# An eight-layer transformer stack: two bias products move from TensorE to VectorE, and the attention behind the expert layer is reordered

## The chip, the cores and the metric

One core of a Trainium2 chip runs the whole program. The metric is device microseconds of one execution, the median of several runs.

## The reference

x has 8 blocks of 128 rows by 512. Eight layers are added to it in turn, each on a layer norm of x. The change lies in the third (L1 attention) and in how it is prepared and started inside the second (L0 expert layer, 4 of 16 experts a row and one shared).

```python
x = x + _L0_xattn_ref(_layernorm(x), ctx_4096, mask, ...)
x = x + _L0_ffn_ref(_layernorm(x), ...)            # 16 experts, top 4, a shared expert
x = x + _L1_xattn_ref(_layernorm(x), ctx_4096, L1_xattn_Wq, L1_xattn_bq, L1_xattn_Wk, L1_xattn_bk)
...
def _L1_xattn_ref(text, features, Wq, bq, Wk, bk):
    Q = jnp.einsum('btx,dx->btd', text, Wq) + bq
    K = jnp.einsum('bpx,dx->bpd', features, Wk) + bk
    scale = 1.0 / jnp.sqrt(K.shape[-1])
    attn = jax.nn.softmax(jnp.einsum('btd,bpd->btp', Q, K) * scale, axis=-1)
    return jnp.einsum('btp,bpd->btd', attn, features)
```

## The kernel before

The function `l0_ffn` (L777) holds the expert layer and the L1 attention behind it, in one block with a hand-written order for each engine; semaphores tie them together. x stays in SBUF. On trn2's TensorE a product of exact f32 is written as one `pe.matmul` and shows as two instructions; elsewhere three products of split parts (`matmul_split`, L239) stand for one.

**Ahead of the loop.** The shared expert is computed (`job`, `down`), while VectorE routes rows: `send(b)` makes one-hot rows and `add(b)` (L1217) adds a block of the shared expert's result. `down` (L1490) waits for `add` of the block but one before and calls `join(c, d)` (L1589) after each block. Four joins, of four products each, make Wk^T Wq, 512 by 512, in PSUM banks 0 to 3; the first two run before `down`. `tokens` (L1534) turns the one-hots into lists; VectorE makes gather and scatter indices of them. `join_vec` (L1601) multiplies both weights with the other's bias: 72 matmuls of one column (Wk bq, Wq bk, bk bq); ScalarE takes them (`take_vec`). Then `tile_turn(0)` waits for rows gathered by GpSimd (`gather`, L1177).

**The tile loop.** 47 tiles of 128 rows of one expert each. Step t on TensorE: `tile_gu(t)` (12 split products), `tile_turn(t+1)`, `tile_down(t-1)` (L1577), `tile_turn_z(t)`. ScalarE: silu(t), the copy of turned rows t+1, the upper part of the weights of t+2 (`tile_gu_hi`, which waits for their load), the output of t-1. VectorE: z(t), rests of rows t+1, zt(t), rest of the weights of t+2 (`tile_gu_lo`), and from t = 21 on, in 18 steps, one step of the quantisation of the next layer's weights (`quantise_weights`, L1417). GpSimd gathers rows of t+3 and scatters picks of t-2. SP (L966 to L1021) issues all plain loads on one queue in the order below; `load_gu` is conditional: a tile with the expert of the one before loads nothing.

```python
for t in range(F0_BUFS, F0_TILES):      # F0_BUFS = 3, F0_TILES = 47
    load_gu(t)                          # 1 MB, waits for t_gu_lo_ready of t - 3
    if t > F0_BUFS: load_dn(t - 1)      # 0.5 MB, waits for t_y_done of t - 4
    if t == 2 * F0_BUFS: ...            # waits for the joins, then a_ct (2 MB, ctx_turned)
    if t == 4 * F0_BUFS: ...            # a_rows (2 MB, ctx_rows)
    if t == 6 * F0_BUFS: ...            # the next layer's weights and columns, 1.75 MB (prefetch)
```

**Behind the loop.** Keys of a half of the blocks are five products (`keys(n, c)`, n = 5 half + m; the fifth is the row of bias terms) of the joined matrix with ctx_turned. The five of half 0 come first. The four picks of each block are loaded into three 1 MB buffers, and `add_pick` adds them; statistics (`ahead.dve`), variance and power on GpSimd, `rows(b)` (the normalised block, two buffers), `turn_rows`, `scores`, `maxima`, `exponentials`, `turn_e`, `attend` (L1665), `add_attended` with the next norm's statistics. These run in a pipeline of ten steps; the 20 chunks of half 1's keys stand in its first four steps, five in each (`late_keys`), between the other work of TensorE. After the last rstd comes a barrier, then the next layer.

Of the kernel before, what the change touches and what calls it, by code (L numbers as in the profile page):

```python
# [12 lines left out]
B = 8  # L13
# [763 lines left out]
def l0_ffn(core):  # L777
    nc, dram, ps = core.nc, core.dram, core.psum
    with ExitStack() as lay:
# [149 lines left out]
        a_bias = sbuf(nc, lay, "a1_bias", [P, 2, NC])  # L929
# [4 lines left out]
        a_xn = t_dn[:, 2, :, :]  # L934
        a_row, a_ones = logit[0:1, :], before_f[0:1, P:2 * P]
        a_w_loaded = [core.sem(f"a1_w_loaded_{i}") for i in range(2)]
        a_bias_loaded, prefetched = core.sem("a1_bias_loaded"), core.sem("f0_prefetched")
        a_joined_done, a_joined_ready = core.sem("a1_joined_done"), core.sem("a1_joined_ready")
        a_vec_done, a_vec_ready = core.sem("a1_vec_done"), core.sem("a1_vec_ready")
# [8 lines left out]
        VEC_BANK, XT_BANK, JOB_BANK, S_BANK, ET_BANK, A_BANK = 7, 0, 2, 4, 5, 6  # L948
# [5 lines left out]
        with nc.Block(no_gpsimd_drain=True) as block:  # L954
            @block.sync
            def _(sp):
# [29 lines left out]
                sp.dma_start(a_bias[:, :, :], dram["a1_bias"]).then_inc(a_bias_loaded, 16)  # L986
# [9 lines left out]
                for t in range(F0_BUFS, F0_TILES):  # L996
# [3 lines left out]
                    if t == 2 * F0_BUFS:  # L1000
                        sp.wait_ge(a_joined_done, NC)
                        sp.wait_ge(a_vec_done, 1)
                        for h in range(HALVES):
                            sp.dma_start(a_ct[:, h, :, :].rearrange("p c n -> p (c n)"), dram["ctx_turned"][h])\
                              .then_inc(a_ct_loaded[h], 16)
                    if t == 4 * F0_BUFS:
# [3 lines left out]
                    if t == 6 * F0_BUFS:  # L1010
# [13 lines left out]
            def _(act):  # L1024
# [43 lines left out]

                def take_vec():

                    act.wait_ge(a_vec_done, 1)
                    act.mul(a_vec[:, 0:2 * NC], ps[:, VEC_BANK, 0:2 * NC], a_scale).then_inc(a_vec_ready, 1)
                    act.mul(a_vec[0:1, 2 * NC:], ps[0:1, VEC_BANK, 2 * NC:2 * NC + 1], a_scale)\
                       .then_inc(a_vec_ready, 1)
# [60 lines left out]
                take_vec()  # L1135
# [10 lines left out]
                for n in range(KEY_JOBS):  # L1146
                    take_keys(n)
                for s in range(1, B + 2):
                    if s >= 2:
                        exponentials(s - 2)  # L1150
                        take_turned(s - 2)
                    if s <= B:
                        take_rows(s - 1)
                    if s <= HB:
                        take_keys(KEY_JOBS + s - 1)
                    if s == HB:
                        take_keys(KEY_JOBS + s)

            @block.gpsimd
            def _(pool):  # L1160
# [39 lines left out]
                for s in range(B + 2):  # L1200
                    if s < B:
                        ahead.scale(pool, s)
                    if s >= 2:
                        late.scale(pool, s - 2)
# [4 lines left out]
            def _(dve):  # L1209
# [149 lines left out]
                def rows(b):  # L1359
# [3 lines left out]
                    if b >= 2:  # L1363
                        dve.wait_ge(a_turned, b - 1)
                    dve.tensor_scalar(a_xn[:, b % 2, :], core.x[:, b, :], ahead.mean(b), ahead.rstd(b),
# [49 lines left out]
                Q_FROM = 7 * F0_BUFS  # L1415
# [35 lines left out]
                for t in range(F0_TILES):  # L1451
# [4 lines left out]
                    if t + 2 < F0_TILES:  # L1456
                        tile_gu_lo(t + 2)
                    quantise_weights(t)
                for s in range(B + 2):
                    if s < B:  # L1460
                        dve.wait_ge(picks_loaded[s], 16)
                        add_pick(s, 0)
                        add_pick(s, 1)
                    if 1 <= s <= B:
                        rows(s - 1)
                    if s < B:
                        add_pick(s, 2)
                        add_pick(s, 3)
                        dve.wait_ge(picks_added, F0_TOPK * (s + 1))
                        ahead.dve(dve, s)  # L1470
                    if s >= 2:
                        add_attended(s - 2)
                    if 1 <= s <= B:
                        maxima(s - 1)
# [1819 lines left out]
```

## Time and profile before

| | us |
|---|---|
| median of 3 runs (1162.65 to 1171.52) | 1163.18 |
| the profiled execution | 1166.7 |
| its span | 1164.9 |
| TensorE busy in the span | 969.0 |
| VectorE busy | 723.1 |
| ScalarE busy | 459.6 |
| GpSimd busy | 393.1 |

The execution's time is taken around the span; the 1.8 us between them lie outside what the profile shows. Busy shares are means over stages with different bounds. Start times below count from the span's start. PE is TensorE, DVE VectorE, ACT ScalarE, POOL GpSimd, SP the engine that issues loads. In square brackets stands the idle time just before an instruction and what ended it.

### The profile page before, as it was taken

The page shows a single profiled execution, that of the slowest core. Times are in us where ns is not written, and L with a number is a line of the kernel's source. Part 1 is how long each engine was busy: PE and PEld are TensorE (multiplying, and loading weights), DVE is VectorE, ACT ScalarE, POOL GpSimd, SP SyncE. Part 2 cuts the span into 40 slices and gives each one's busy share as a digit, 9 for nine tenths or more (in the row PEclk, how much of TensorE's full clock was granted, in tenths as well). Part 3 has the DMA queues.
Part 4 walks back from the last instruction along what each step waited for, and adds up shares of the span by engine and source line. Part 5 has one row for each costly group of instructions (what it writes and reads, how often), then busy time and mean ns, then how long its engine had stood idle before and what let it go on. Part 6 is the DMA issues. An engine that isn't in the chain of part 4 may idle for free. (4 is left out here: it accounts for less than half of the span.)

```text
span 1164.9 us, 15202 instructions
## 1 busy us (share of the span) xinstructions
PE 969.0 (83%) x5083; PEld 643.6 (55%) x5083; DVE 723.1 (62%) x1183; ACT 459.6 (39%) x671; POOL 393.1 (34%) x355
## 2 busy tenths in 40 slices
PE   4888766999999999999734389899986588769997
PEld 2565533786666666654412168544463255457886
DVE  4767464675776778736859744477744667544434
ACT  2445323224666566632232143344402256335130
POOL 5334111213676666631112640100011231227531
PEclk8899675988999999999855579799988889979999
DMA  8000103134888866545100131000001020022000
GB/s 301 1 2 2 55 0 133 42 148 138 317 313 317 288 228 244 204 143 195 55 0 1 44 119 37 19 2 1 1 1 73 37 82 0 1 72 91 19 19 37
DMA packets 31982, 110.09 MB, mean 95 GB/s; under 512 B 4321, under 2 KB 4641, under 8 KB 28577
## 3 DMA queue, kind: packets, MB, share of 16 engines
q1 hardware_dynamic: 24384, 84.47, 20.0%
q0 software_dynamic: 7520, 24.65, 6.0%
q8 instruction: 42, 0.69, 0.2%
q14 instruction: 36, 0.29, 0.1%
HBM read 130.07 MB, written 16.78 MB: 126 GB/s over the span
## 5 line engine op out<-in xcount | busy, mean ns | idle before, releaser
L1186 POOL DMA_INDIRECT f_picks<-f_turn_xn,f_target x47 | 116.4, 2477 | 71.5 <-ACT f_turn_xn L1063 71.2
L1585 PE MATMUL banks<-f_t_dn,f_z 128*128 128x512 f32 x188 | 88.5, 593 | 0.6 <-issue 0.6
L1328 DVE TENSOR_TENSOR f_gu_lo<-f_t_gu,f_gu_hi 128x2048 fp32r<-128x2048 f32 x24 | 55.0, 2293 | 15.1 <-ACT f_gu_hi L1049 14.2
L1180 POOL DMA_INDIRECT f_turn_xn<-f_xn_rows,f_token x47 | 47.4, 1008 | 50.1 <-DVE f_token L1322 21.4
L106 POOL TENSOR_TENSOR a_ahead_var_eps<-mean_var,eps 128x1 f32<-128x1 f32 x24 | 4.8, 199 | 176.0 <-DVE mean_var L102 176.0
L1328 DVE TENSOR_TENSOR f_xn_lo<-f_t_gu,f_xn_hi 128x2048 fp32r<-128x2048 f32 x23 | 52.7, 2292 | 10.7 <-ACT f_xn_hi L1049 10.3
L2255 ACT ACTIVATE a_e<-banks 128x1024 f32<-128x1024 f32 x32 | 32.8, 1024 | 52.8 <-PE banks L2354 52.7
L1049 ACT CAST f_gu_hi<-f_t_gu 128x2048 fp32r x24 | 45.7, 1904 | 11.9 <-DMA f_t_gu<-in_f_gu 9.0
L1056 ACT ACTIVATE f_sil<-banks 128x256 f32<-128x256 f32 x47 | 18.1, 384 | 80.1 <-PE banks L244 80.1
L164 PE MATMUL banks<-ident,f_turn_xn 128*128 128x128 f32 x96 | 21.3, 374 | 33.9 <-DVE f_turn_xn L172 33.9
L100 DVE BATCH_NORM_STATS2 stat<-x_res 128x6 f32<-128x512 f32 x64 | 44.3, 692 | 5.5 <-DMA x_res<-in_x 3.5
L1049 ACT CAST f_xn_hi<-f_t_gu 128x2048 fp32r x23 | 43.7, 1901 | 7.2 <-DMA f_t_gu<-in_f_gu 5.1
L1585 PEld LDWEIGHTS banks<-f_t_dn,f_z 128*128 128x128 f32 x188 | 32.1, 190 | 23.3 <-issue 23.2
L453 ACT ACTIVATE a_e<-banks 128x1024 f32<-128x1024 f32 x32 | 31.0, 1021 | 35.4 <-PE banks L661 35.4
L421 POOL TENSOR_TENSOR a_k<-a_kf,a_k_sel 128x512 fp32r<-128x512 f32 x16 | 20.8, 1302 | 68.8 <-ACT a_k_sel L445 68.8
L2292 DVE TENSOR_REDUCE a_mx<-banks 128x8 f32<-128x1024 f32 x32 | 39.1, 1222 | 7.2 <-PE banks L2336 5.9
L242 PE MATMUL banks<-f_gu_hi,f_xn_hi 128*128 128x512 f32 x96 | 41.0, 427 | 1.9 <-issue 1.9
L542 DVE TENSOR_REDUCE a_mx<-banks 128x8 f32<-128x1024 f32 x32 | 37.6, 1218 | 5.3 <-PE banks L644 5.3
L1333 DVE TENSOR_TENSOR f_xn_lo<-banks,f_xn_hi 128x512 fp32r<-128x512 f32 x47 | 32.4, 690 | 11.9 <-ACT f_xn_hi L1041 11.5
L2368 PE MATMUL banks<-a_e,raw 128*32 128x512 f32 x128 | 35.4, 631 | 4.6 <-DVE a_ot_lo L2284 4.6
L242 PE MATMUL banks<-f_xn_hi 128*128 128x512 f32 x92 | 38.2, 415 | 1.0 <-issue 1.0
L243 PE MATMUL banks<-f_gu_lo,f_xn_hi 128*128 128x512 f32 x96 | 39.0, 406 | 0.0
(437 smaller groups left out, 2705.9 us busy)
## 6 DMA issues: line engine op xcount, KB each, us to landing
f_t_gu<-in_f_gu SPq DMA_DIRECT2D x47, 1024.0 KB
f_t_dn<-in_f_dn SPq DMA_DIRECT2D x47, 512.0 KB, 4.3
f_t_gu<-f_picks SPq DMA_DIRECT2D x8, 1024.0 KB, 5.4
f_xn_rows<-f_turn_xn SPq DMA_DIRECT2D x9, 256.0 KB, 2.5
x_res<-in_x SPq DMA_DIRECT2D x8, 256.0 KB, 8.3
a_ctx<-in_ctx SPq DMA_DIRECT2D x2, 1024.0 KB, 13.8
a_out_mask<-in_mask SPq DMA_DIRECT2D x1, 2048.0 KB, 16.0
a_ct<-in_ctx_turned SPq DMA_DIRECT2D x2, 1024.0 KB, 11.3
```

Source lines behind the costliest of these rows:

```text
L100: dve.bn_stats(self.stat[:, b, :], src).then_inc(self.stat_ready, 1)
L242: pe.matmul(out, w_hi, m_hi, start=start, stop=False)
L243: pe.matmul(out, w_hi, m_lo, start=False, stop=False)
L542: dve.tensor_reduce(mx[:, :, PAIR * (s % 2) + A0_MAX_ROW:PAIR * (s % 2 + 1):A0_SLOT].rearrange("p w r -> p r w"), ps[:, s_banks(s), :].rea ...
L1049: act.copy(t_gu_hi[t % 2], t_gu[:, bass.ds(i, 1), :, :].rearrange("p i c n -> p (i c n)"))\
L1180: pool.indirect_dma_start(t_rows[:, t % F0_BUFS, :], None, dram["f0_xn_rows"], bass.IndirectOffsetOnAxis(ap=token[:, t:t + 1], axis=0))\
L1186: pool.indirect_dma_start(dram["f0_picks_flat"], bass.IndirectOffsetOnAxis(ap=target[:, t:t + 1], axis=0), t_y[:, t % F0_BUFS, :], None).t ...
L1328: dve.tensor_tensor(t_gu_lo[t % 2], t_gu[:, bass.ds(i, 1), :, :].rearrange("p i c n -> p (i c n)"), t_gu_hi[t % 2].bitcast(F32), ALU.subtr ...
L1585: mm = pe.matmul(ps[:, TY_BANK + t % 2, :], t_zt[:, t % 2, c, :], t_dn[:, t % F0_BUFS, c, :], start=c == 0, stop=c == F0_IC - 1)
L2255: act.activation(e[:, u % 2, 2 * (s % 2):2 * (s % 2) + 2, :], ps[:, s_bank(s):s_bank(s) + 2, :], ACT.Exp, scale=scale).then_inc(exp_ready, 1)
L2292: dve.tensor_reduce(mx[:, tiles, A2_MAX_ROW:P:A2_SLOT].rearrange("p m r -> p r m"), ps[:, s_bank(s):s_bank(s) + 2, :].rearrange("p r (m j) ...
L2368: mm = pe.matmul(ps[A2_VSLOT * i:A2_VSLOT * (i + 1), O_BANK + u % 2, :], v[:, b // HB, b % HB, g * A2_PER_GROUP + i, :], e[:, u % 2, i, :] ...
```

## The change

- The bias products: SP loads both weights turned, wk and wq (1 MB each), into `raw`, and the two biases repeated over all partitions (0.5 MB) into the room of a_rows, all at t = 6 in front of a_ct. VectorE multiplies and sums in nine instructions (`join_biases`) in tiles t = 9 to 17. `join_vec` and `take_vec` go.
- The joins of chunks 2 and 3 move from `down` to behind `tokens`.
- a_rows is loaded at t = 21 instead of 12, once all nine are done; the prefetch at 21 instead of 18; the quantisation starts at t = 24 instead of 21.
- Behind the loop TensorE makes all ten keys in one go. VectorE adds the picks of six blocks meanwhile; `rows` has six buffers (all of t_dn) instead of two. Then come nine steps, the first eight of them with a block's scores.

```diff
@@ -926,17 +926,19 @@
         a_wk, a_wq = (core.raw[:, i, :].rearrange("p (c n) -> p c n", c=NC) for i in range(2))
-        a_bias = sbuf(nc, lay, "a1_bias", [P, 2, NC])
+        a_turned_w = core.raw[:, :, :].rearrange("p i (c n) -> p i c n", c=NC)
+        a_bias = a_rows[:, 0, 0:2, :]
         a_vec = sbuf(nc, lay, "a1_vec", [P, 2 * NC + 1])
...
         a_inv = sbuf(nc, lay, "a1_inv", [P, B])
-        a_xn = t_dn[:, 2, :, :]
+        a_xn = t_dn[:, :, :, :].rearrange("p i c n -> p (i c) n")
+        A_XN = F0_BUFS * F0_IC
...
@@ -983,7 +985,6 @@
 
-                sp.dma_start(a_bias[:, :, :], dram["a1_bias"]).then_inc(a_bias_loaded, 16)
                 sp.wait_ge(gu_lo_ready, 1)
...
@@ -999,15 +1000,18 @@
                         sp.wait_ge(a_joined_done, NC)
-                        sp.wait_ge(a_vec_done, 1)
+                        for i, w in enumerate(("a1_wk_turned", "a1_wq_turned")):
+                            sp.dma_start(core.raw[:, i, :], dram[w]).then_inc(a_turned_loaded, 16)
+                        sp.dma_start(a_bias, dram["a1_bias"]).then_inc(a_turned_loaded, 16)
                         for h in range(HALVES):
...
                               .then_inc(a_ct_loaded[h], 16)
-                    if t == 4 * F0_BUFS:
+                    if t == 7 * F0_BUFS:
+                        sp.wait_ge(a_vec_ready, 2 * NC + 1)
                         for h in range(HALVES):
...
                               .then_inc(a_rows_loaded[h], 16)
-                    if t == 6 * F0_BUFS:
+                    if t == 7 * F0_BUFS:
                         for i, src in enumerate(core.upcoming):
...
@@ -1132,7 +1129,6 @@
                 tile_x(0)
-                take_vec()
                 for t in range(F0_TILES):
...
@@ -1143,18 +1139,14 @@
 
-                for n in range(KEY_JOBS):
+                for n in range(HALVES * KEY_JOBS):
                     take_keys(n)
-                for s in range(1, B + 2):
-                    if s >= 2:
-                        exponentials(s - 2)
-                        take_turned(s - 2)
-                    if s <= B:
-                        take_rows(s - 1)
-                    if s <= HB:
-                        take_keys(KEY_JOBS + s - 1)
-                    if s == HB:
-                        take_keys(KEY_JOBS + s)
+                take_rows(0)
+                for s in range(B):
+                    exponentials(s)
+                    if s + 1 < B:
+                        take_rows(s + 1)
+                    take_turned(s)
 
...
@@ -1197,11 +1189,13 @@
                 pool.drain()
-                for s in range(B + 2):
-                    if s < B:
-                        ahead.scale(pool, s)
-                    if s >= 2:
-                        late.scale(pool, s - 2)
+                for b in range(A_XN):
+                    ahead.scale(pool, b)
+                for s in range(B + 1):
+                    if s + A_XN < B:
+                        ahead.scale(pool, s + A_XN)
+                    if s >= 1:
+                        late.scale(pool, s - 1)
 
...
@@ -1360,9 +1354,9 @@
                         dve.wait_ge(t_y_done, F0_TILES)
-                    if b >= 2:
-                        dve.wait_ge(a_turned, b - 1)
-                    dve.tensor_scalar(a_xn[:, b % 2, :], core.x[:, b, :], ahead.mean(b), ahead.rstd(b),
+                    if b >= A_XN:
+                        dve.wait_ge(a_turned, b - A_XN + 1)
+                    dve.tensor_scalar(a_xn[:, b % A_XN, :], core.x[:, b, :], ahead.mean(b), ahead.rstd(b),
                                       ALU.subtract, ALU.mult).then_inc(a_xn_ready, 1)
...
@@ -1412,7 +1406,20 @@
 
-                Q_FROM = 7 * F0_BUFS
+                def join_biases(t):
+
+
+                    n = t - 3 * F0_BUFS
+                    if n == 0:
+                        dve.wait_ge(a_turned_loaded, 48)
+                    if 0 <= n <= 2 * NC:
+                        i, c = divmod(n, NC)
+                        one = a_turned_w[:, i, c, :] if i < 2 else a_bias[:, 0, :]
+                        dve.scalar_tensor_tensor(out=turned.xn[:, B - 1, :], in0=one, scalar=a_scale,
+                                                 in1=a_bias[:, min(i, 1), :], op0=ALU.mult, op1=ALU.mult,
+                                                 accum_out=a_vec[:, n:n + 1]).then_inc(a_vec_ready, 1)
+
+                Q_FROM = 8 * F0_BUFS
 
...
@@ -1455,23 +1462,28 @@
                         tile_gu_lo(t + 2)
+                    join_biases(t)
                     quantise_weights(t)
-                for s in range(B + 2):
+                def all_picks(b):
+                    dve.wait_ge(picks_loaded[b], 16)
+                    for k in range(F0_TOPK):
+                        add_pick(b, k)
+                    dve.wait_ge(picks_added, F0_TOPK * (b + 1))
+                    ahead.dve(dve, b)
+
+                all_picks(0)
+                for b in range(1, A_XN):
+                    all_picks(b)
+                    rows(b - 1)
+                for s in range(B + 1):
+                    if s + A_XN < B:
+                        all_picks(s + A_XN)
+                    if s + A_XN - 1 < B:
+                        rows(s + A_XN - 1)
                     if s < B:
-                        dve.wait_ge(picks_loaded[s], 16)
-                        add_pick(s, 0)
-                        add_pick(s, 1)
-                    if 1 <= s <= B:
-                        rows(s - 1)
-                    if s < B:
-                        add_pick(s, 2)
-                        add_pick(s, 3)
-                        dve.wait_ge(picks_added, F0_TOPK * (s + 1))
-                        ahead.dve(dve, s)
-                    if s >= 2:
-                        add_attended(s - 2)
-                    if 1 <= s <= B:
-                        maxima(s - 1)
+                        maxima(s)
+                    if s >= 1:
+                        add_attended(s - 1)
 
...
@@ -1500,7 +1512,6 @@
                         mm.then_inc(y_done, 1)
-                        join(2 + b // NC, b % NC)
 
...
@@ -1598,28 +1607,13 @@
 
-                def join_vec():
-
-
-                    pe.wait_ge(a_bias_loaded, 16)
-                    pe.wait_ge(sigmoid_ready, 1)
-                    for i, w in enumerate((a_wk, a_wq)):
-                        for c in range(NC):
-                            for d in range(NC):
-                                pe.matmul(ps[:, VEC_BANK, i * NC + c:i * NC + c + 1], w[:, d, c * P:(c + 1) * P],
-                                          a_bias[:, 1 - i, d:d + 1], start=d == 0, stop=d == NC - 1)
-                    for d in range(NC):
-                        mm = pe.matmul(ps[0:1, VEC_BANK, 2 * NC:2 * NC + 1], a_bias[:, 1, d:d + 1],
-                                       a_bias[:, 0, d:d + 1], start=d == 0, stop=d == NC - 1)
-                    mm.then_inc(a_vec_done, 1)
-
                 def keys(n, c):
...
                             pe.wait_ge(a_joined_ready, NC)
-                            pe.wait_ge(a_vec_ready, 2)
+                            pe.wait_ge(a_vec_ready, 2 * NC + 1)
                             pe.wait_ge(t_z_ready, F0_TILES)
...
@@ -1687,7 +1681,9 @@
                 tokens()
-                join_vec()
+                for c in range(2, NC):
+                    for d in range(NC):
+                        join(c, d)
                 pe.wait_ge(y_added, B)
...
@@ -1700,28 +1696,19 @@
 
-                for n in range(KEY_JOBS):
+                for n in range(HALVES * KEY_JOBS):
                     for c in range(NC):
                         keys(n, c)
-                def late_keys(s, a, b):
-
-                    if s <= HB:
-                        for i in range(KEY_JOBS * (s - 1) + a, KEY_JOBS * (s - 1) + b):
-                            keys(KEY_JOBS + i // NC, i % NC)
-
-                for s in range(1, B + 2):
-                    if s >= 2:
-                        turn_e(s - 2)
-                    late_keys(s, 0, 1)
-                    if s >= 2:
-                        attend(s - 2)
-                    late_keys(s, 1, 2)
-                    if s <= B:
-                        turn_rows(s - 1)
-                    late_keys(s, 2, 3)
-                    if s <= B:
-                        scores(s - 1)
-                    late_keys(s, 3, KEY_JOBS)
+                turn_rows(0)
+                for s in range(B + 1):
+                    if s < B:
+                        scores(s)
+                    if s + 1 < B:
+                        turn_rows(s + 1)
+                    if s >= 1:
+                        attend(s - 1)
+                    if s < B:
+                        turn_e(s)
         core.next = 1 - core.next
...
@@ -3175,7 +3162,8 @@
     out["a1_wk"], out["a1_wq"] = rows(a["L1_xattn_Wk"]), rows(a["L1_xattn_Wq"])
-    out["a1_bias"] = np.stack([a["L1_xattn_bk"].reshape(NC, P).T, a["L1_xattn_bq"].reshape(NC, P).T], 1)
+    out["a1_wk_turned"], out["a1_wq_turned"] = rows(a["L1_xattn_Wk"].T), rows(a["L1_xattn_Wq"].T)
+    out["a1_bias"] = np.broadcast_to(np.stack([a["L1_xattn_bq"], a["L1_xattn_bk"]]), (P, 2, D))
     out["f1_w"] = a["L1_ffn_W"].reshape(NC, P, D).transpose(1, 0, 2).reshape(P, NC * D)
...
         [a[f"L1_ffn_{key}"] for key in ("calib_min", "calib_max", "bias")]), (P, 3 * D))
```

## Rows read from the trace of the kernel before

**Rows 1.** The page: TensorE's clock in 40 slices of 29.1 us.
```profile
PEclk8899675988999999999855579799988889979999
```

**Rows 2.** Windows: us, each engine's busy us, then clock, DMA share, GB/s.
```profile
249.00:262.00 13.00, 13.00 (x102) 12.65 (x101) 6.16 (x9) 1.77 (x4) 4.73 (x3) 0.68 0.19 61
262.00:515.00 253.00, 248.34 (x1042) 170.63 (x1042) 180.20 (x205) 153.72 (x187) 158.09 (x90) 0.98 0.68 246
...
580.00:600.00 20.00, 10.98 (x43) 6.12 (x41) 8.49 (x20) 3.68 (x10) 3.68 (x10) 0.67 0.00 0
```

**Rows 3.** TensorE's timeline ahead of the loop: start us, us, line, operation.
```profile
248.52 1.02 PE L1596 MATMUL banks<-raw 128*128 128x512 f32 x2
249.38 1.56 PE L1538 MATMUL banks<-f_sent,f_at_row 128*128 128x94 bf16 x32
250.78 11.21 PE L1609 MATMUL banks<-a_bias,raw 128*128 128x1 f32 x64
...
262.19 1.12 PE L1550 MATMUL banks<-ident,f_turn_xn 128*128 128x128 f32 x4
264.75 0.77 PE L242 MATMUL banks<-f_gu_hi,f_xn_hi 128*128 128x512 f32 x1 [1.45 <-issue]
```

**Rows 4.** Timeline of VectorE and GpSimd there; landings of ten gathers.
```profile
246.48 0.69 DVE L1219 TENSOR_TENSOR x_res<-banks,x_res 128x512 f32<-128x512 f32 x1
...
248.72 0.69 DVE L1219 TENSOR_TENSOR x_res<-banks,x_res 128x512 f32<-128x512 f32 x1
...
253.27 1.24 POOL L1180 DMA_INDIRECT f_turn_xn<-f_xn_rows,f_token  x1 [21.39 <-DVE f_token L1322]
...
DMA to landing us min/median/max: 3.2/3.7/8.5
```

**Rows 5.** Windows of one us, clock before the DMA share.
```profile
270.00:271.00 1.00, 0.93 (x5) 0.65 (x3) 0.34 (x1) 0.42 (x2) 0.00 (x0) 0.67 0.00 0
```

**Rows 6.** Landings of a_ct's two loads, of load_dn(6), and TensorE's tile_down(6).
```profile
L1004 SPq DMA_DIRECT2D a_ct<-in_ctx_turned x2: 432/454/475, 288.5 to 289.0; - x2
...
DMA to landing us min/median/max: 9.3/11.3/13.2
...
L982 SPq DMA_DIRECT2D f_t_dn<-in_f_dn x1: 342/342/342, 293.2 to 293.2; - x1
...
DMA to landing us min/median/max: 11.2/11.2/11.2
...
306.63 1.88 PE L1585 MATMUL banks<-f_t_dn,f_z 128*128 128x512 f32 x4
```

**Rows 7.** VectorE's timeline at t = 21: a quantisation step, then z.
```profile
385.40 0.68 DVE L1395 TENSOR_REDUCE f_weights_scale<-raw 128x1 f32<-128x512 f32 x1
386.12 0.42 DVE L1341 TENSOR_TENSOR f_z<-f_sil,banks 128x256 f32<-128x256 f32 x1
```

**Rows 8.** Timeline of ScalarE at the loads of t = 24 and 25.
```profile
387.62 1.91 ACT L1049 CAST f_gu_hi<-f_t_gu 128x2048 fp32r x1 [1.74 <-DMA f_t_gu<-in_f_gu]
...
393.35 1.91 ACT L1049 CAST f_xn_hi<-f_t_gu 128x2048 fp32r x1 [2.04 <-DMA f_t_gu<-in_f_gu]
```

**Rows 9.** Timeline behind the loop, all engines.
```profile
515.24 13.90 PE L1632 MATMUL banks<-a_ct,a_joined 128*128 128x512 f32 x32
...
524.93 3.11 DVE L1355 SCALAR_TENSOR_TENSOR x_res<-f_t_gu,f_weight,x_res 128x512 f32<-128x512 f32 x4 [11.58 <-DMA f_t_gu<-f_picks]
...
528.07 0.69 DVE L100 BATCH_NORM_STATS2 stat<-x_res 128x6 f32<-128x512 f32 x1
...
573.83 2.04 PE L1654 MATMUL banks<-f_turn_xn,a_xt 128*128 128x128 f32 x8 [0.72 <-issue]
...
588.74 1.13 PE L1654 MATMUL banks<-f_turn_xn,a_xt 128*128 128x128 f32 x8 [0.72 <-issue]
...
589.80 0.48 PE L1656 MATMUL banks<-f_logit,f_before_f 1*128 1x128 f32 x2
...
596.09 0.54 POOL L109 TENSOR_TENSOR rstd<-second_ahead_var_eps,neg_half 128x1 f32<-128x1 f32 x1
```

## What the change was predicted to do

> **What bounds the kernel now.** First the page's slices, then one table of the windows of each stage, then the timeline of each place where the change cuts in. The clock row of the slices (29.1 us each) [rows 1] reads 8 from 233 to 291, 9 up to 553, then 8 and 5. The windows tell which work that is [rows 2]: in the loop (262 to 515) TensorE is busy 248.3 of 253 us at a clock of 0.98, with the DMA engines at 0.68. It is the bound there, but only because data comes in time. In 580:600 it is busy 11 of 20 us at 0.67, where steps wait on one another. In 249:262 it is "full", but of tiny matmuls, and mostly at half clock (1.2 of 2.4 GHz). So four stretches count: the lead to the loop, two bursts of DMA in it, and the steps behind it. What lies after 597 is not touched.
>
> **Part 1, ahead of the loop: -8.2 us (0 to -9).** join_vec's L1609 starts at 250.78 and takes 11.2 us, and the first turn starts at 262.19 with no idle before it [rows 3]. That and L1612's last 0.3 us go. The eight joins of chunks 2 and 3 move from `down` to behind `tokens`: 16 instructions (two to a product) at 0.43 us, from two in the 0.86 us between L1596's start at 248.52 and L1538's at 249.38 [rows 3], so 6.9 us. In `down` they cost nothing to take out and give nothing but the last pair: VectorE's round of `send` and `add` is 248.72 - 246.48 = 2.24 us [rows 4], as long as TensorE's with the joins, so VectorE sets the pace without them. The last pair goes from in front of `tokens`: 0.86 us, so tokens end at 250.1 and the joins at 257.0. The first gather starts at 253.27 - 0.86 = 252.4; gathers land in 3.2 us at best, 3.7 in the median [rows 4], so by 256.1, under the joins. Turn, ScalarE's copy, VectorE's rest: 262.19 to 264.75 at half clock [rows 3], some 2.1 us at full. tile_gu(0) starts at 259.1 instead of 264.75: -5.7. If the clock holds, a second gain: the half clock lasts until about 270.7 [rows 5], so gu(0)'s 5.3 us become 2.8: -2.5. Upper bound 0: in `down` TensorE now has idle time (1.4 us of work in 2.24), and if the clock falls there, the joins take 13.8 us.
>
> **Part 2, the burst at t = 6: +9.5 us (+5 to +12).** SP issues wk, wq turned (1.05 MB each), the biases (0.52 MB) and then the same ctx_turned; all on SP's one queue, ahead of load_dn(6). ctx_turned's two 1.05 MB pieces, issued 0.48 us apart, land in 9.3 and 13.2 us [rows 6]: 4.4 us apart, 240 GB/s. load_dn(6), issued at 293.21 behind them, lands in 11.2 us [rows 6], at 304.4. It is read by tile_down(6) at 306.63 [rows 6]: 2.2 us of slack. 2.62 MB more at 240 GB/s is 10.9 us: it lands at 315.3, 8.7 us late. TensorE then stands, gathers and scatters stop and the queue gets their share: I take 7 us. Skipped loads of gate and up weights (t = 7 to 10, same expert) issue nothing; the next real one, t = 11, comes after the backlog. I expect the clock to fall in a stand of 7 us; at the loop's start it stayed at half from 264.75 to 270.7 [rows 3, 5], and each us at half clock loses 0.5: +2.5.
>
> **Part 3, nine products on VectorE, t = 9 to 17: 0 (0 to +5).** Each is put where a step of the weights' quantisation stands later: behind gu_lo, before z. Such a step took 0.68 us and z began at 386.12 [rows 7]; TensorE turned that z without waiting, at 386.8, 0.27 us after z's end. So up to 0.95 us is free. The nearest operation, a scalar_tensor_tensor of 512, is 0.75 us ([rows 9]: 3.11 us for four, overlapped). With an accumulator it isn't in this trace; bounds 0.75 and twice it.
> The Trainium skill (Vector Engine (DVE) Microarchitecture Reference, section 7, Points that are easy to get wrong) says that such an instruction with two non-bf16 sources in SBUF runs at half throughput, both read ports being taken and none left for the accumulator. The four adds have two such sources and show no halving; with an accumulator no run here shows it. By the rule these nine would be 1.5 us and the time 1169.
> The quantisation moves by three tiles; it starts at t = 24, long behind its load. The keys now wait for all nine products and tile_down(1) for none; they are done at t = 17, so neither counts.
>
> **Part 4, the burst at t = 21: +9 us (+4 to +14).** ctx_rows (2.1 MB, was t = 12) and the prefetch (1.83 MB, was t = 18) go out together at about 365.9, just ahead of three real loads of gate and up weights in a row (t = 23, 24, 25). Even before, the engines were behind there: ScalarE waits 1.74 and 2.04 us for the loads of t = 24 and 25, which land at 387.6 and 393.3 [rows 8]. SP's new wait for the ninth product, behind which all later weight loads stand, costs nothing: load_dn(20), just ahead of it, waits for a later tile. Up to the load of t = 25 the queue now has 0.52 + 3.93 + 3 x (0.52 + 1.05) = 9.2 MB from 365.9. At 240 GB/s that is 38 us; two loads landed 5.75 us apart with 1.57 MB between [rows 8], 273 GB/s. I take 270, as a standing TensorE frees the engines: 34 us and, an estimate, 1.4 of latency, landing at 401.3 instead of 393.3: +8. The quantisation step that stood behind it (0.68) is gone, and the load of t = 20 no longer queues behind the prefetch: -1, an estimate. The clock after a stand of 8 to 10 us: +2. The move of ctx_rows from t = 12 gives back nothing, no tile was late there.
>
> **Part 5, behind the loop: -9.6 us (-11.6 to +5.4).** The keys: before, 40 instructions from 515.24 at 0.43 us [rows 9], then 40 more in gaps. Now all 80: 34.2 us, to 549.5. VectorE meanwhile: picks from 524.93; a block is 3.14 + 0.73 + 0.1 = 3.95 us ([rows 9]: 3.11 for four, statistics at 528.07), rows() 0.46. Seven blocks and six rows(): 524.9 + 27.7 + 2.8 = 555.4; there comes maxima(0), after scores(0) (552.6). Picks land in time: three buffers, so 13.2 us for a load that takes 4.4 us at the rate of [rows 6] and some latency. Table load, exponential: scores(1) starts at 557.9. TensorE has stood 4.3 us, so I take half clock till 563. Last block, rows(6), rows(7), add_attended(0): maxima(2) at 565.5. From there a step at full clock is on TensorE: scores 1.5 (588.74 to 590.28 [rows 9]), attend two instructions of 0.43, turn and turn_e some 0.75 (four transposes took 1.12 at half clock [rows 3]) = 3.1 us; VectorE has 0.75 + 0.9 for sum and statistics as in a block, some 0.5 for maxima and reciprocal, and waits for attend between. I take 3.25. Scores(7) end at 581.6. From the end of scores(7) to the layer's last rstd was 590.28 to 596.63 = 6.35 us with attend at half clock [rows 9]; 5.3 at full. End 587.0 against 596.6. Lower bound: no fall at all, 585. Upper: half clock throughout (L1654 2.04 us instead of 1.13 [rows 9]), a step 5.9: 602.
>
> **Sum.** -8.2 + 9.5 + 0 + 9 - 9.6 = +0.7. The profiled execution took 1166.7 us (span 1164.9, 1.8 around it), 3.5 over the median of the runs, 1163.18. 1166.7 + 0.7 = 1167.4 in its frame, 1163.9 against the median; I say 1164.
>
> **Rivals.**
> A: the bursts cost nothing, because later weights overtake them. The load of 11.2 us [rows 6] speaks against it, a TensorE that hardly idles in the loop [rows 2] for it. -8.2 - 9.6, and about 2 us of lateness that before had [rows 8]: 1143. Half hidden: 1153. Chance 0.15.
> B, slower: the clock stays at half in the eight steps. Place: from 557 on; price: 5.9 instead of 3.25 us a step, +15, to 1179; it decides if the idle time of 580:600 [rows 2] comes back. For it: that row. Against: the new step leaves TensorE next to no idle time. Chance 0.12.
> C: the clock falls in `down` or both bursts go at 240 GB/s with no help from stopped gathers: +6 to +14, 1170 to 1178. Chance 0.2.
> D: the products with an accumulator take 1.5 us: z is late 0.55 us in each of nine tiles, +5: 1169. Chance 0.08.
> Forecast (the two halves cancel within 8 us): 0.45.
>
> **How the numbers follow.** This kernel's measurement can tell about 1% (11.6 us) from no change. Faster by more (under 1151.5) is most of A: 0.15. Slower by more (over 1174.8) is B and half of C: 0.22. The rest 0.63. Range: the forecast is good to +-8; it reaches half of A's way and through most of C: 1152 to 1177.
>
> **What would show it.** TensorE's first gu at about 259 at full clock. Load_dn(6) landing after 20 us or more and tile_down(6) standing about 7 us for it; none at t = 12. ScalarE waiting 8 us or more for f_t_gu near t = 23. The loop as long as 253 + 14 us. Keys in one block of 34 us, maxima(0) about 40 us behind its start, then steps of 3.3 us. Wrong if the loop's tiles keep 5.17 us throughout, or if steps are over 5 us.

## The result: 0.8% faster, where no change was forecast

The changed kernel takes 1160.88 us (median of 20 runs, 1152.3 to 1166.65), the kernel before 1167.76 on the same chips (20 runs, 1162.65 to 1174.27; of the three runs known beforehand, median 1163.18, two were at its low end). The ratio is 0.9924, 95% interval [0.9905, 0.9943]: 6.9 us faster by the medians, 8.9 by the ratio. That is inside the range forecast and inside the 1%, but the balance forecast was +0.7 us, and what came is a gain clear of the noise.

The profiled execution has a span of 1159.2 us against 1164.9. Windows of the changed kernel (us; busy us of each engine; clock, DMA share, GB/s), beside [rows 2]:

```profile
246.00:255.00 9.00, 7.50 (x23) 3.42 (x21) 6.60 (x10) 1.66 (x3) 5.62 (x4) 1.00 0.24 66
255.00:262.00 7.00, 5.99 (x28) 4.59 (x28) 2.23 (x4) 2.88 (x3) 0.99 (x2) 1.00 0.35 103
262.00:518.00 256.00, 243.10 (x1003) 166.31 (x1002) 181.33 (x219) 150.12 (x181) 154.71 (x88) 0.97 0.71 251
292.00:308.00 16.00, 10.31 (x34) 6.70 (x33) 6.03 (x5) 3.80 (x6) 4.49 (x3) 0.79 0.75 293
380.00:396.00 16.00, 9.43 (x30) 6.10 (x29) 6.27 (x6) 6.22 (x8) 6.16 (x4) 0.79 0.88 363
518.00:553.00 35.00, 35.00 (x82) 13.25 (x80) 23.66 (x38) 6.76 (x10) 8.02 (x11) 1.00 0.73 253
557.00:572.00 15.00, 12.40 (x40) 8.95 (x41) 9.75 (x22) 3.71 (x12) 2.85 (x6) 0.55 0.01 2
```

The half clock ahead of the loop is gone. TensorE idles in two stretches of the loop, 292 to 308 and 380 to 396, and works at half clock from 557 to 572.

**Ahead of the loop.** TensorE's timeline of the changed kernel (start us, us), beside [rows 3]:

```profile
243.61 1.39 PE L1549 MATMUL banks<-f_sent,f_at_row 128*128 128x94 bf16 x28
245.72 0.35 PE L1549 MATMUL banks<-f_sent,f_at_row 128*128 128x94 bf16 x4 [0.72 <-DVE f_sent L1299]
245.91 7.10 PE L1605 MATMUL banks<-raw 128*128 128x512 f32 x16
252.85 0.60 PE L1561 MATMUL banks<-ident,f_turn_xn 128*128 128x128 f32 x4
254.94 0.47 PE L242 MATMUL banks<-f_gu_hi,f_xn_hi 128*128 128x512 f32 x1 [1.50 <-issue]
```

VectorE's timeline, two of its rounds, beside [rows 4]:

```profile
243.49 0.68 DVE L1213 TENSOR_TENSOR x_res<-banks,x_res 128x512 f32<-128x512 f32 x1
...
245.58 0.68 DVE L1213 TENSOR_TENSOR x_res<-banks,x_res 128x512 f32<-128x512 f32 x1
```

A round of `down` is now 2.09 us, not 2.24. Most of `tokens` (28 of 32 matmuls) runs while VectorE prepares the last block, the joins follow at once, and the gather lands under them: TensorE stands 0.72 us for VectorE, not at all for the gather, and its clock doesn't fall.

**Burst 1.** SP's timeline, then TensorE's:

```profile
275.89 0.48 SPq L1004 DMA_DIRECT2D raw<-in_a_wk_turned  x1
276.42 0.86 SPq L1004 DMA_DIRECT2D raw<-in_a_wq_turned  x1
277.33 0.63 SPq L1005 DMA_DIRECT2D a_rows<-in_a_bias  x1
278.00 1.78 SPq L1007 DMA_DIRECT2D a_ct<-in_ctx_turned  x2
281.84 0.11 SPq L976 DMA_DIRECT2D f_t_gu<-in_f_gu  x1
282.71 0.34 SPq L984 DMA_DIRECT2D f_t_dn<-in_f_dn  x1
```

```profile
293.68 0.60 PE L1561 MATMUL banks<-ident,f_turn_xn 128*128 128x128 f32 x4
299.97 3.78 PE L1594 MATMUL banks<-f_t_dn,f_z 128*128 128x512 f32 x4 [5.69 <-DMA f_t_dn<-in_f_dn]
...
307.71 0.60 PE L1561 MATMUL banks<-ident,f_turn_xn 128*128 128x128 f32 x4
```

load_dn(6), issued at 282.71, is what tile_down(6) waits 5.69 us for. It then runs at half clock (3.78 us, 1.88 in [rows 6]). From the start of one turn to the next it is 14.03 us where a plain tile has 5.16: +8.9.

**Burst 2.** SP's first issue of it, then ScalarE's timeline, beside [rows 8], then TensorE's:

```profile
362.35 2.95 SPq L1012 DMA_DIRECT2D a_rows<-in_ctx_rows  x2
```

```profile
384.66 1.90 ACT L1053 CAST f_xn_hi<-f_t_gu 128x2048 fp32r x1 [8.40 <-DMA f_t_gu<-in_f_gu]
...
388.32 1.90 ACT L1053 CAST f_gu_hi<-f_t_gu 128x2048 fp32r x1 [0.51 <-DMA f_t_gu<-in_f_gu]
...
396.39 1.90 ACT L1053 CAST f_xn_hi<-f_t_gu 128x2048 fp32r x1
```

```profile
380.23 0.60 PE L1561 MATMUL banks<-ident,f_turn_xn 128*128 128x128 f32 x4
...
389.38 0.69 PE L1584 MATMUL banks<-ident,f_z 128*128 128x128 f32 x2 [5.76 <-DVE f_z L1335]
...
395.06 0.60 PE L1561 MATMUL banks<-ident,f_turn_xn 128*128 128x128 f32 x4
```

The first of the three loads in a row comes 8.4 us late and stops TensorE by way of z; the third is in time (396.39, no wait), but it is asked for later too, since the tiles ahead of it had stood. Turn to turn 14.83 us: +9.7. The small lateness of the kernel before at t = 20 to 25 (6.15, 5.42, 6.50 and 5.71 us a tile, 3.1 in all) is gone in exchange.

**Behind the loop.** TensorE's timeline, beside [rows 9]:

```profile
518.61 13.90 PE L1626 MATMUL banks<-a_ct,a_joined 128*128 128x512 f32 x32
...
556.31 0.66 PE L1636 MATMUL banks<-ident,f_t_dn 128*128 128x128 f32 x4
559.56 0.47 PE L1657 MATMUL banks<-ident,a_e 128*128 128x128 f32 x1 [2.59 <-ACT a_e L1099]
560.08 2.05 PE L1648 MATMUL banks<-f_turn_xn,a_xt 128*128 128x128 f32 x8
...
565.60 1.92 PE L1648 MATMUL banks<-f_turn_xn,a_xt 128*128 128x128 f32 x8
...
571.00 1.66 PE L1648 MATMUL banks<-f_turn_xn,a_xt 128*128 128x128 f32 x8
...
574.47 1.13 PE L1648 MATMUL banks<-f_turn_xn,a_xt 128*128 128x128 f32 x8
...
577.57 1.13 PE L1648 MATMUL banks<-f_turn_xn,a_xt 128*128 128x128 f32 x8
```

Each of these is a block's scores. The steps are 5.5 and 5.4 us at half clock (560.08, 565.60, 571.00) and 2.9 to 3.1 at full.

### The profile page after: what moved, and what is told of

Its sections match the earlier page's. It is cut to its first block and busy times, and to the rows that moved or that the text cites. A ratio compares the mean times of both kernels' runs of the same rounds, so it can differ in the third digit from the quotient of the medians.

```text
span 1159.2 us, 15070 instructions
## 1 busy us (share of the span) xinstructions
PE 954.2 (82%) x5011; PEld 631.8 (55%) x5011; DVE 726.1 (63%) x1201; ACT 459.0 (40%) x669; POOL 395.4 (34%) x355
## 5 line engine op out<-in xcount | busy, mean ns | idle before, releaser
L1342 DVE COPY f_z<-banks 128x256 f32<-128x256 f32 x47 | 20.0, 425 | 33.7 <-PE banks L1584 33.6
L2979 DVE TENSOR_TENSOR f_square<-f_relu 128x512 f32<-128x512 f32 x16 | 19.5, 1224 | 31.0 <-ACT f_relu L2922 25.9
```

## One table for all runs

To compare fourteen executions, each span is cut at four points of TensorE's timeline: the first matmul of `down`, the turn of tile 1, the first product of the keys, the end of the last attend. Head, loop and behind are the stretches between them. Ahead of `down` no kernel here differs from another, but for one small load, of the biases, that only the kernel before and e7 have there.

| kernel | down starts | head | loop | behind | time, us (runs) | ratio to before |
|---|---|---|---|---|---|---|
| before | 231.0 | 38.97 | 245.23 | 78.70 | 1167.76 (20) | 1 |
| before, again | 236.5 | 39.29 | 246.21 | 80.09 | 1174.83 (1) | |
| changed | 228.9 | 28.90 | 260.78 | 69.25 | 1160.88 (20) | 0.9924 |
| changed, again (e5) | 233.7 | 28.90 | 259.79 | 65.52 | 1157.65 (10) | 0.9905 |
| e1 burst 1 spread | 235.9 | 28.91 | 251.59 | 68.26 | 1157.7 (7) | 0.9913 |
| e6 the same, again | 230.5 | 28.91 | 253.67 | 66.71 | 1154.4 (4) | 0.9859 |
| e2 burst 2 spread | 228.2 | 28.91 | 249.27 | 66.88 | 1147.07 (6) | 0.9834 |
| e3 both spread | 235.6 | 28.91 | 243.23 | 66.85 | 1143.33 (6) | 0.9782 |
| e4 joins in down | 233.2 | 33.28 | 257.15 | 65.51 | 1165.21 (12) | 0.9978 |
| e7 part 5 alone | 237.1 | 36.06 | 245.74 | 66.64 | 1156.05 (4) | 0.9881 |
| e8 e3 + 12 matmuls | 230.5 | 28.90 | 245.72 | 71.35 | 1149.8 (4) | 0.9846 |
| e11 e3 + 6 matmuls | 235.7 | 28.91 | 243.45 | 66.21 | 1143.35 (4) | 0.9794 |
| e10 e3 + early scores | 231.1 | 28.90 | 244.63 | 68.41 | 1145.1 (6) | 0.9827 |
| e12 e3 + products twice | 237.8 | 28.91 | 247.27 | 66.97 | 1148.94 (4) | 0.9841 |

The times come from several chips. The kernel before, taken beside each, had medians of 1168.66 (e1 to e4), 1167.66 (e5 to e8) and 1164.29 us (e9 to e12), and the ratio is to that one. The second row is a single run.

What follows the last attend is 570.5 to 571.8 us in all of them. The start of down varies by 9.6 us from one execution to the next, the same kernel's by 4.7 (changed) and 5.5 (both e1's and before's). So two traces can't be compared by their spans: the two shown differ by 5.7 us, of which 2.1 lie ahead of the change. Cut up and averaged over two executions each, the change is -10.2 in the head, +14.6 in the loop, -12.0 behind it: -7.6, and the medians say -6.9.

## Experiments

**e1 to e3: the two bursts spread out.** e1's edit (a name in brackets stands for its dma_start):

```
 if t == 2 * F0_BUFS:
     sp.wait_ge(a_joined_done, NC)
-    (wk_turned, wq_turned, a_bias, ctx_turned[0], ctx_turned[1])
+    (wk_turned)
+if t == 2 * F0_BUFS + 1: (wq_turned)
+if t == 2 * F0_BUFS + 2: (a_bias)
+if t == 4 * F0_BUFS + h: (ctx_turned[h])      # h = 0, 1
```

e2's edit:

```
-if t == 7 * F0_BUFS: wait a_vec_ready; (ctx_rows[0], ctx_rows[1]); (upcoming[0], upcoming[1])
+if t == 26: sp.wait_ge(a_vec_ready, 2 * NC + 1)
+if t == 26 + i: (upcoming[i])                 # i = 0, 1
+if t == 28 + h: (ctx_rows[h])
-Q_FROM = 8 * F0_BUFS
+Q_FROM = 29
```

Expected of e1:

> The changed kernel, with the first burst spread out: wk_turned stays at t = 6, wq_turned goes to t = 7, the biases to t = 8, ctx_turned's two pieces to t = 12 and 13, in tiles without a load of gate and up weights. Theory (load_dn(6) stood behind 4.7 MB): tile_down(6) no longer waits, the 14.03 us tile becomes 5.2, no half clock there, time 8 to 9 us under the changed kernel's, 1152. Rival (DMA engines are simply full there, whatever the order): the wait reappears in tiles 7 to 13 in smaller pieces, and the gain is 0 to 4 us.

Of e2:

> The changed kernel, with the second burst moved and spread out: the two prefetched pieces at t = 26 and 27, ctx_rows' two at t = 28 and 29, and the quantisation from t = 29 instead of 24. Theory (3.9 MB stood ahead of three real loads of gate and up weights): the 14.83 us tile and ScalarE's 8.4 us wait go; since the kernel before was already 3.6 us late at these three loads, part of that may stay or go too: gain 9 to 10 us over the changed kernel, 1151. Rival (half of it is owed to the three loads themselves): about 5 us remain at t = 24 and 25, gain 5 us.

Of e3, both edits:

> Both of the edits above together. Theory (two independent stalls): the gains add, 17 to 19 us under the changed kernel, about 1142, and the tile loop takes 47 tiles of 5.17 us and some 2 us at most. Rival (a queue that is full moves its delay elsewhere): less than 12 us.

Measured: in e1 the 14.03 us tile is plain, one later tile has 5.55, and the loop is 9.2 us shorter. In e2 the 14.83 us tile and ScalarE's long wait are gone, the loop 11.5 shorter, 13.8 us by the medians. That is more than the 9 to 10 expected, but 2.9 of the 11.5 are burst 1's tile, which took 11.13 us here instead of 14.03; burst 2's own part is 8.6. In e3 no tile is over 5.62 us, the loop takes 243.23, 2.0 less than in the kernel before, and the time is 1143.33, ratio 0.9782 [0.9753, 0.9812]. Window of e3 beside the loop's in [rows 2] (e3's loop itself ends at 507.7, where its keys begin):

```profile
262.00:515.00 253.00, 251.06 (x1047) 170.92 (x1046) 183.13 (x222) 154.48 (x187) 157.45 (x90) 1.00 0.74 260
```

The DMA engines are busier than in [rows 2] (0.74 against 0.68), TensorE idles less and its clock stays up. The same bytes, asked for in other tiles, cost nothing: the rival of engines that are simply full is refuted. No run moved a burst without spreading it, so which of the two helps more is not shown. Both edits together gain 17.5 us of the changed kernel's median (14.3 of e5's, 17 and 14 by the ratios), as the theory of two separate stalls had it, and beat both kernels: 25 us under the kernel before by the ratio.

e1's time disagreed with its trace: 3 us under the changed kernel where the trace had lost 9. Hence e5 and e6.

**e5, e6: the changed kernel and e1 again,** with no edit.

> The changed kernel once more, unedited, for the parts that vary from one execution to the next. The four kernels of the first call began down between 228.2 and 235.9 us, though nothing ahead of it differs, and their stretch behind the loop took 65.5 to 69.3 us. If these are chance, this run's head (start of down to turn of tile 1) is again 28.9 us, the 6th tile's stall between 5 and 9 us over a plain tile, the stretch behind the loop 65 to 70, and the start of down anywhere in 228 to 236. If the differences belong to each kernel, this one begins down at 228.9 and takes 69.3 behind the loop again.

> The kernel with the first burst alone spread out, once more, beside the unedited changed kernel on the same chip. Its trace lost the stall of tile 6 (loop 251.6 instead of 260.8 us) but its median was only 3 us under the changed kernel's, and down began 7 us later in it. If that late start was chance: down begins at 229 to 233 here, and the time is 6 to 9 us under the changed kernel's in this call. If it belongs to this kernel, down begins at 236 again and the time is 2 to 3 us under.

Measured: head 28.90 and 28.91 to the hundredth; down at 233.66 and 230.48 where it had been at 228.9 and 235.9; behind the loop 65.52 and 66.71. So the start and the length of the stretch behind the loop vary by chance, in one kernel. Burst 1's tile took 12.78 us here, 14.03, 11.13 (e2) and 10.75 (e4) in the others: its stall is 5.6 to 8.9 us, 7 in the mean. e6 is 3.3 us under the changed kernel again, by 4 runs and with intervals of some 0.8%: less than the 6 to 9 expected, but these few runs can't tell the two apart. By the loops of the table (260.3 and 252.6 in the mean of two) it is 7.7. Burst 1's worth in time is open between 3 and 8 us.

**e4: the joins back in down.** Edit:

```
 mm.then_inc(y_done, 1)
+join(2 + b // NC, b % NC)
 ...
 tokens()
-for c in range(2, NC):
-    for d in range(NC):
-        join(c, d)
```

> The changed kernel, with the eight joins of chunks 2 and 3 back in down, one behind each block. Step of my prediction under test: VectorE sets the pace of down, so the joins cost nothing there; then rounds stay at 2.1 us, tokens end 0.9 us later for the last pair, and the gathers alone set the first turn. New theory: TensorE sets it with the joins; rounds are 2.24 instead of 2.09 us, tokens end some 1.9 us later than in the changed kernel, the first turn comes 0 to 1 us later because the gather of 3.2 us is no longer covered. Both say time within 1 us of the changed kernel; the trace's rounds tell them apart.

VectorE's timeline of e4, its last two adds, then TensorE's:

```profile
248.60 0.69 DVE L1213 TENSOR_TENSOR x_res<-banks,x_res 128x512 f32<-128x512 f32 x1
...
250.84 0.69 DVE L1213 TENSOR_TENSOR x_res<-banks,x_res 128x512 f32<-128x512 f32 x1
```

```profile
251.50 1.56 PE L1550 MATMUL banks<-f_sent,f_at_row 128*128 128x94 bf16 x32
259.10 1.08 PE L1562 MATMUL banks<-ident,f_turn_xn 128*128 128x128 f32 x4 [6.04 <-DMA f_turn_xn<-f_xn_rows,f_token]
```

Rounds are 2.24 us again, so TensorE with the joins sets them; VectorE alone needs 2.09. But both theories missed the size: 4.3 us slower (1165.21), as the head says (33.28 against 28.90). TensorE stands 6.04 us for the gather, the clock falls to half (the turn 1.08 us, not 0.60), and tile 0 takes 7.34 us instead of 4.98. Joins behind `tokens` instead of in `down` are worth this: they fill the wait for the gather.

**e7: part 5 alone.** The kernel before with the change's edits to a_xn and A_XN, to the order behind the loop on all four engines, and no other.

> The kernel before, with part 5 of the change alone: all 80 instructions of the keys in one go, six blocks of picks ahead, eight short steps. My prediction's step gives -9.6 us, 1158 against 1167.8. Theory now: keys' start to the last attend takes 65 to 70 us instead of 78.7, by how long the half clock lasts after TensorE's stand of 5.3 us; time 9 to 13 us under the kernel before. Rival (the gain needs the turned loads or the joins of the change): under 5 us. Head 39.0 and loop 245.2 us as in the kernel before.

Measured: behind the loop 66.64 us, loop 245.74, time 1156.05, ratio 0.9881 [0.9818, 0.9944]. The stretch behind the loop is 12 to 13.5 us shorter than in the two traces of the kernel before, the median 11.6 under the kernel before on the same chip (1167.66). Part 5 works by itself. Its head was 36.06, not 38.97, though nothing is changed there. TensorE's timeline, beside L1609 in [rows 3]:

```profile
256.87 9.11 PE L1612 MATMUL banks<-a_bias,raw 128*128 128x1 f32 x64
```

The same 64 matmuls take 9.11 or 11.21 us, by when in them the clock falls to half: in windows of 1 us it was at 0.50 from 254 in the kernel before, 3 us after their start, and from 262 here, 5 us after it.

**e9: the kernel before again.**

> The kernel before, unedited, for its own variation. Its head (start of down to turn of tile 1) was 38.97 us with join_vec at 11.2 us, and 36.06 in the kernel with part 5 alone, where join_vec took 9.1 because the half clock came later. If that is chance of the clock, the head is anywhere from 36 to 39 here, the loop 245 to 246, the stretch behind it 75 to 79 us. If it is fixed, 38.97, 245.2 and 78.7 again.

Measured, in one run: 39.29, 246.21, 80.09, which is 0.3, 0.2 and 1.1 us beyond the ranges of chance and not the old numbers either. Its loop has late tiles again at t = 20, 23 and 24 (6.25, 5.98, 6.33 us), and three smaller ones elsewhere.

**e8 and e11: filling the stand behind the keys,** on e3:

```
 turn_rows(s + 1)
+if s == 0:
+    pe.wait_ge(t_y_ready, F0_TILES)
+    for i in range(12):        # e11: range(6)
+        pe.matmul(ps[:, A_BANK + 1, :], a_joined[:, 0, 0:P], a_ct[:, 0, 0, :], start=True, stop=True)
```

> The kernel with both bursts spread, and 12 matmuls (128x512, result unused) on TensorE between turn_rows(1) and the wait for the first exponential, where it stood 5.3 us. Theory (that stand costs half a clock behind it): the clock stays at 1.00 from 553 on in the frame of the changed kernel, scores(1) and the steps 1 and 2 take 1.13 and some 4.5 us instead of 2.05 and 5.4, and the stretch behind the loop is 64.5 us or less instead of 66.9. Rival (VectorE's picks of blocks 6 and 7 set these steps): the clock stays up, but the stretch shortens by less than 1 us.

> As the filler before, with 6 matmuls instead of 12: in float32 each is two instructions of 0.43 us, so 12 took 10.3 us and overshot the stand by 5 (scores(1) at 48.6 us behind the keys' start instead of 41.5), while everything behind scores(1) took 22.7 us, not 24.2 to 27.8. Now 5.2 us: scores(1) at 43.4 at the latest, clock 1.00 throughout. Theory (the half clock costs up to 4 us here): stretch behind the loop 64 to 66 us, the same in every execution. Rival (VectorE's picks of blocks 6 and 7 take the place): 66 to 67, no gain over the kernel with both bursts spread (66.9).

Measured: with 12, scores(1) starts 48.61 us behind the keys' start instead of 41.5 and the stretch grows by 4.5: the filler was twice too long, my error of counting. With 6 it is 66.21. Windows of e3, then of e11:

```profile
543.00:549.00 6.00, 2.62 (x17) 1.86 (x15) 5.79 (x12) 2.91 (x6) 2.27 (x4) 0.92 0.00 0
549.00:555.00 6.00, 5.95 (x20) 4.24 (x20) 3.85 (x9) 1.33 (x6) 0.96 (x2) 0.51 0.01 4
```

```profile
543.00:552.00 9.00, 8.23 (x36) 4.87 (x37) 8.65 (x16) 3.63 (x7) 2.27 (x4) 1.00 0.01 2
552.00:574.00 22.00, 21.35 (x115) 13.94 (x113) 14.19 (x38) 7.86 (x27) 5.57 (x14) 1.00 0.00 0
```

The clock stays at 1.00, yet the stretch is within 0.7 us of e3's 66.85 and not under e5's 65.52, where the half clock was short by chance: it ended 2 us behind maxima(1). VectorE is busy 8.65 of 9 us: maxima(1) stands behind the picks of block 7 and comes at 44.97 here, at 44.5 to 44.8 in e3 to e5. From it to the end are 21.2 us at full clock (e11), 21.0 in e5 and up to 24.5 in the changed kernel's long half clock. So the half clock costs 0 to 3.5 us, by chance, and in this order VectorE's picks set a floor near 65.5. The rival was right: without the half clock nothing was gained.

**e10: the first scores early,** on e3: turn_rows(0), scores(0) and turn_rows(1) ahead of the last four products, `maxima(0)` ahead of `all_picks(6)`, ScalarE's order to match.

> The kernel with both bursts spread, and turn_rows(0), scores(0) and turn_rows(1) placed ahead of the last four products of the keys, maxima(0) ahead of the picks of block 6. Theory (after its 40 us of keys TensorE stands 5.3 us only because maxima(0) stands behind the 7th block of picks on VectorE, and the half clock follows from it): maxima(0) comes at 35.7 us behind the keys' start, not 40.1, no stand over 2.5 us, and the stretch behind the loop takes 61 to 64 us instead of 65.5 to 69.3; time 3 us under the kernel with both bursts spread. Rival (VectorE's 8 blocks of 4.4 us set the end whatever the order): the stretch stays at 65 us or more.

Measured: 68.41 behind the loop and 1145.1 in all, ratio 0.9827 against e3's 0.9782, no gain over e3: a miss. TensorE's timeline of e10:

```profile
544.99 1.02 PE L1675 MATMUL banks<-a_rows,a_et 128*128 128x512 f32 x2
550.24 0.33 PE L1665 MATMUL banks<-ident,a_e 128*128 128x128 f32 x1 [4.23 <-ACT a_e L1103]
```

maxima(0) came at 35.75 as meant, but I had left maxima(1) behind the picks of block 7 (549.41, 44.8 us behind the keys' start), so the stand only moved one step on, and the half clock with it. With maxima(1) moved too it wasn't tried.

**e12: each product twice,** on e3, the second into unused space.

> The kernel with both bursts spread, and each of the nine products done twice (a second one into unused space, its sum unused). One takes 0.68 us, 0.61 from start to start with the next operation, and tiles 9 to 17 kept 5.16 us. My prediction's step says 0.95 us a tile is free on VectorE: twice 0.61 is 1.22, so z is late by 0.3 us in each of nine tiles and TensorE waits for it: periods of 5.2 to 5.5, together 0 to 3 us. Rival (VectorE already sets the tile): 0.6 us more in each, 5.5 us together.

VectorE's timeline of e12:

```profile
325.07 0.68 DVE L1422 SCALAR_TENSOR_TENSOR f_turn_xn<-raw,a_rows 128x512 f32<-128x512 f32 x1
325.69 0.08 DVE L1422 DVE_READ_ACCUMULATOR f_turn_xn<-raw,a_rows 128x1 f32 x1
325.69 0.69 DVE L1425 SCALAR_TENSOR_TENSOR f_turn_xn<-raw,a_rows 128x512 f32<-128x512 f32 x1
326.30 0.08 DVE L1425 DVE_READ_ACCUMULATOR f_turn_xn<-raw,a_rows 128x1 f32 x1
326.30 0.41 DVE L1339 TENSOR_TENSOR f_z<-f_sil,banks 128x256 f32<-128x256 f32 x1
```

The loop is 247.27 us against 243.2 to 245.7 in the four other kernels on e3's loads (mean 244.3): +3.0, at the edge of what was expected. Late are the tiles 10, 12, 14, 16 and 18 (6.98, 5.84, 5.81, 5.55 and 5.51 us), not each of nine by 0.6 as the rival had it. Most of tile 10's lateness is a load of weights, not the product, by ScalarE's timeline of e12:

```profile
315.63 1.91 ACT L1057 CAST f_xn_hi<-f_t_gu 128x2048 fp32r x1 [1.50 <-DMA f_t_gu<-in_f_gu]
```

By the medians e12 is 5.6 over e11 on the same chip, more than the trace shows, from four runs each. A first product is free. A second is not in every second tile, where the cover is thus over 0.61 and under 1.22 us, around the step's 0.95; in the other tiles it was free too.

## Why the prediction was off

**Part 1, -8.2: measured -10.2.** Failed step: "In `down` they cost nothing to take out ... so VectorE sets the pace without them". Two engines had the same 2.24 us, and I took the equality for VectorE's own need. VectorE does set the pace without the joins, but at 2.09 us; 2.24 was TensorE's round, as e4 shows with the joins put back. Seven rounds give 1.0 us, and the tokens that now run under VectorE's last round give most of the rest. That the gather would be hidden held; what placing the joins over it is worth (4.4 us, e4) I had not asked. The old head itself also moves with the clock (36.1 in e7, which has the same code there, 39.3 in e9), by more than this error.

**Part 2, +9.5: +8.9 in the trace, 7 in the mean of four.** Place, cause and size held; its two terms came out as 5.7 us of standing (7 forecast) and some 3.2 of half clock behind it (2.5 forecast). load_dn(6) landed 24.1 us after the burst's first issue (27 forecast).

**Part 3, 0: 0.** The nine tiles with a product keep 5.14 to 5.26 us in both traces. The product was 0.68 us plus 0.08 for the accumulator, 0.61 from start to start (e12's rows above). Rival D falls. By the Trainium skill (Vector Engine (DVE) Microarchitecture Reference, section 7) it would have been half as fast; with both sources float32 in SBUF and an accumulator the trace doesn't agree: each took 0.68 us, not 1.5.

**Part 4, +9: +6.6.** The tile lost 9.7 us, but 3.1 us of lateness went. Failed step: the "+8", which I took from the landing of the third load, and the "-1, an estimate", which I gave back. The third load was in time, 34.0 us at most behind the burst's first issue (35.4 forecast). It was the first of the three, 8.4 us late, that stopped TensorE. While TensorE stood, the other two caught up (the second was 0.5 us late, the third not at all), so this one stop took the place of the old lateness of 3.1 us, of which I had given back only 1. Together the bursts were put at 18.5 us; the loop is 14.6 longer.

**Part 5, -9.6: -9.5 in the two traces shown, -12.0 in the mean.** Keys in one block (34.8 us), maxima(0) 40.1 us behind their start, a stand of TensorE and a half clock: all as forecast. Mis-sized terms: a step 3.0 us, not 3.25 (over five steps 1.2 us); the half clock, taken to end 47.8 us behind the keys' start, ended at about 54 in the first trace and 46 in the second (e5), by chance; and the kernel before, put at its one trace's 78.7, took 80.1 the next time.

So the mechanisms of parts 2, 3 and 5 held, in parts 1 and 4 a step failed, and three terms erred to the same side: 2 + 4 + 2.4 us make up the 8 between +0.7 and -7.6. That 1160.88 lies only 3 us from the 1164 forecast is in part luck: 1164 was counted from a median of 1163.18, and from the 1167.76 of 20 runs the same sum gives 1168.5. Rival A (bursts that cost nothing, 1143) was wrong of the changed kernel. Its case, a loop without stalls, is e3, at 1143.33, but by spreading the loads and not because later weights overtake them; that the numbers agree is luck, since A's sum is 20 us and e3's gain 25. B happened in small, two steps of 5.4 to 5.5 us, and C not at all.

## What to carry to other kernels

Loads that are prefetched into a loop cost by where they stand in the queue, not by their bytes alone: place each behind the last urgent load of a run and ahead of tiles that need none (here 14 to 17.5 us from moving eight of them). When two engines show the same period, find out what each needs alone before taking work off one of them. Work that nobody waits for is best put where its engine would wait for a transfer, since there it also keeps the clock up.

## What was not expected of the hardware

In one kernel the time ahead of the change varied by up to 5.5 us from execution to execution, over all fourteen by 9.6. The granted clock differs there too. In the windows from 35 to 55 us it was 0.99 and 1.00 in the kernel before, which begins `down` at 231.0, and 0.57 and 0.67 in e1, which begins it at 235.9:

```profile
35.00:45.00 10.00, 8.41 (x119) 5.80 (x121) 6.03 (x9) 4.87 (x7) 4.27 (x3) 0.99 0.01 2
45.00:55.00 10.00, 8.74 (x131) 6.37 (x123) 7.47 (x12) 6.57 (x9) 1.82 (x2) 1.00 0.01 2
```

```profile
35.00:45.00 10.00, 9.22 (x81) 6.82 (x81) 5.34 (x8) 3.13 (x4) 4.83 (x3) 0.57 0.01 2
45.00:55.00 10.00, 8.79 (x77) 5.68 (x77) 5.46 (x8) 3.81 (x5) 1.27 (x1) 0.67 0.01 2
```

The same work draws a fall of the clock in one execution and none in another; that this is the whole of the 4.9 us is not shown. And issuing was slow in a burst: the two ctx_rows issues took 2.95 us of SP's queue, against 0.91 for the same two alone at t = 12 in the kernel before.
